# Layer 1's experts in two phases by choice, with residual and gates carried in the token's row, and shorter routing

## The reference

```python
gate_logits = x_flat @ Wg + bg + bias
topk_vals, topk_idx = jax.lax.top_k(gate_logits, 2)
topk_w = jax.nn.softmax(topk_vals, axis=-1)
h = relu(einsum('td,edh->teh', x_flat, W1) + b1)     # 256 -> 512
y = einsum('teh,ehd->ted', h, W2) + b2               # 512 -> 256
out = sum over the two chosen experts of topk_w * y
x = x + out
```

## Time and profile before

| what | value |
|---|---|
| runs without profile, us | 1401.55, 1405.42, 1402.47; median 1402.47 |
| the profiled execution's own time, us | 1402.67 |
| its span in the profile, us | 1400.8 |
| mean granted PE clock in the span, as a share of full | 0.828 |
| busy in the span: PE, DVE, POOL, ACT | 76%, 69%, 56%, 37% |
| layer 1's experts, first to last PE instruction, us from the start | 925 to 1325 |
| the combine after them | 1326 to the end |

### The profile page before, as it was taken

One profiled execution on the slowest core, in us unless ns is written; L12 is line 12 of the kernel. 1 busy time (PEld: TensorE's weight loads), 2 busy tenths in 40 slices (PEclk: granted clock), 3 DMA queues, 4 the chain that ended last, 5 costly groups with the idle time before them and its releaser, 6 DMA issues.

```text
span 1400.8 us, 30856 instructions
## 1 busy us (share of the span) xinstructions
PE 1061.8 (76%) x9022; PEld 875.1 (62%) x9023; DVE 965.6 (69%) x1758; ACT 520.3 (37%) x1067; POOL 784.7 (56%) x807
## 2 busy tenths in 40 slices
PE   5989756379999993667786481679999999999700
PEld 4767545248888882455564370459888888889600
DVE  3788689957777773578896798845555555555377
ACT  2656464802222221457676574012222222222200
POOL 3466755026666645777731375047777777777300
PEclk9999855559999997688888555569999999999955
DMA  9311124015555554333320253012222222223199
GB/s 284 56 46 39 61 95 146 0 30 159 165 165 165 165 143 128 87 112 114 117 61 31 90 171 115 1 57 91 93 91 90 90 91 93 94 90 93 52 356 363
DMA packets 121953, 157.13 MB, mean 112 GB/s; under 512 B 26904, under 2 KB 102176, under 8 KB 121632
## 3 DMA queue, kind: packets, MB, share of 16 engines
q1 hardware_dynamic: 96160, 86.05, 18.9%
q0 software_dynamic: 25728, 70.29, 17.0%
HBM read 95.47 MB, written 60.82 MB: 112 GB/s over the span
## 4 chain that ended last, share of the span: by engine, by line
PE 55%; issue 16%; DVE 12%; POOL 8%; DMA 4%; ACT 3%; SPq 1%; DVEq 0%; POOLq 0%; ACTq 0%
PE bank L814 19%; PE bank L828 19%; PE bank L785 5%; PE bank L797 4%; PE bank L663 4%; POOL WREG L534 3%; DMA arena<-expert_outputs 2%; DVE stats L1090 1%; DVE X L1100 1%; DVE X L1171 1%; SPq L306 1%; PE bank L691 1%; PE bank L681 1%; DVE X L1178 1%; POOL arena L542 1%
## 5 line engine op out<-in xcount | busy, mean ns | idle before, releaser
L605 POOL DMA_INDIRECT arena<-split_tokens,gather_row x272 | 282.0, 1037 | 233.9 <-DVE gather_row L1434 117.9
L1009 ACT ACTIVATE arena<-bank,b1T 128x256 f32<-128x256 f32 (+1 forms) x432 | 167.2, 462 | 497.1 <-PE bank L814 497.1
L828 PE MATMUL bank<-WREG,arena 128*128 x2448 | 289.8, 273 | 11.4 <-issue 5.2
L814 PE MATMUL bank<-arena,WREG 128*128 128x256 f16 (+1 forms) x2592 | 296.3, 269 | 0.0
L828 PEld LDWEIGHTS bank<-WREG,arena 128*128 128x128 f16 x2448 | 235.7, 98 | 47.5 <-issue 19.4
L814 PEld LDWEIGHTS bank<-arena,WREG 128*128 x2592 | 239.9, 99 | 26.5
L1446 DVE CAST arena<-arena 128x512 f16<-128x512 f32 (+1 forms) x136 | 78.7, 578 | 230.9 <-ACT arena L1009 230.9
L614 POOL DMA_INDIRECT expert_outputs<-arena,scatter_row x136 | 155.1, 1141 | 63.9 <-issue 40.6
L663 PE MATMUL bank<-wg_sb,arena 128*128 128x258 f32 x512 | 140.7, 422 | 41.4 <-ACT arena L874 33.6
L534 POOL DMA_INDIRECT WREG<-expert_outputs,pos_i x128 | 125.8, 983 | 61.0 <-issue 38.0
L663 PEld LDWEIGHTS bank<-wg_sb,arena 128*128 128x128 f32 x512 | 101.8, 208 | 65.3 <-issue 37.3
(11 more groups left out here) (190 smaller groups left out, 1343.4 us busy)
## 6 DMA issues: line engine op xcount, KB each, us to landing
expert_outputs<-arena SPq DMA_DIRECT2D x68, 256.0 KB, 2.8
split_tokens<-arena SPq DMA_DIRECT2D x32, 512.0 KB, 2.9
arena<-expert_outputs SPq DMA_DIRECT2D x32, 512.0 KB, 8.0
X<-in_x SPq DMA_DIRECT2D x16, 512.0 KB, 6.0
stage_w<-in_L_ffn_W SPq DMA_DIRECT2D x16, 512.0 KB, 3.4
out<-X SPq DMA_DIRECT2D x16, 512.0 KB, 8.0
arena<-split_tokens,gather_row POOLq DMA_INDIRECT x272
stage_w<-in_L_ffn_w SPq DMA_DIRECT2D x16, 256.0 KB, 2.8
```

The costliest lines, as they stand in the source:

```text
L605: nc.gpsimd.indirect_dma_start(out=gat[:, u * 512:(u + 1) * 512], out_offset=None, in_=table[L], in_offset=bass.IndirectOffsetOnAxis(ap=ga ...
L814: last = mm(hb, w1_at(L, ea, wh, kc, fc), tT[:, tb:tb + width], start=n == 0, stop=n == 3 * KC - 1)
L828: last = mm(ob[a], hsrc[:, h0:h0 + P], w2_at(L, e[a % len(e)], wh, fc), start=fc == 0 and n == 0, stop=fc == FC - 1 and n == 2)
L1009: ins = A(hid[:, h0:h0 + width], bank[2 + 2 * (u % 2) + fc // 2][:, b0:b0 + width], ACT.Gelu if L == 0 else ACT.Relu, bias=cut(b1T, ea * F ...
```

## The change

In both layers routing is trimmed: masks in float16, both choices' positions handled in one instruction where that can be (`pos_both`), one instruction instead of six from the matmuls' result to `gather_row`. The register loads of the slots' experts become one load for each slot, and the turn in layer 1 is eight slots long.

In layer 1 the two choices are routed apart. All first choices are one list (phase 0) and all second choices another (phase 1), each with room for 32 whole and 4 mixed slots: 72 slots, 144 tiles. Each token has one row of 2056 bytes in DRAM: the two float16 halves of y (1024 bytes), the residual x (1024 bytes) and the two gates (8 bytes). SP stores x into `token_rows_0` during the attention, y after the second layernorm; ACT stores the gates (8192 pieces of 8 bytes). In phase 0 a slot's rows are gathered from `token_rows_0` into a ring of 8 slots, which takes the place of X in SBUF; PE transposes the y part; when `copy_out` is done, DVE adds gate times output to the residual in the row (`add_to_row`, two instructions for a slot), and POOL scatters the whole row to `token_rows_1`. Phase 1 gathers from there, adds the second choice and scatters 1024 bytes to the result. There is no combine. Phase 1's rows can only be gathered when phase 0 is written (`phase_written`); for its first seven slots a second gather from `token_rows_0` (`fetch_early`) gives PE the y part sooner.

The diff, cut to what the prediction speaks of:

```diff
@@ constants
+PHASES = (1, TOPK)
+BIG = [TOKENS * TOPK // SLOT // n for n in PHASES]      # 64, 32
+RUN = [n + MIXED for n in BIG]                          # 68, 36
+SLOTS = [n * m for n, m in zip(PHASES, RUN)]            # 68, 72
+TURN = (SU, 2 * SU)
+ROW = 2 * D + TOPK
+RING = 2 * SU
+EARLY = 7
@@ def of_slots
-            eng.reg_load(regs, cut(table, first, len(regs)))
+            for f, r in slots:
+                mixed = isinstance(r, int) and r >= BIG[L]
+                key = f * KEYS[L] + (BIG[L] + ST * (r - BIG[L]) if mixed else r)
+                found.append([next(regs) for _ in range(ST if mixed else 1)])
+                eng.reg_load(found[-1], cut(table, key, len(found[-1])))
@@ SP
-        def load_outputs(sp, L):
...
+                def store_x(g):
+                    sp.wait_ge(x_done[1], at(4 * g + 4))
+                    sp.dma_start(rows_of(0)[:, g * GT:(g + 1) * GT, D:2 * D],
+                                 xs(g * GT, GT).rearrange("p (t d) -> p t d", d=D)).then_inc(x_stored, 16)
@@ POOL, layer 1
-                for t in range(AHEAD_G):
-                    gather(t)
-                for t in range(STILES):
-                    if t + AHEAD_G < STILES:
-                        gather(t + AHEAD_G)
-                    if L == 1:
-                        scatter(t)
+                def fetch(s):
+                    f, j = s // RUN[1], s % RING
+                    if s >= RING:
+                        pool.wait_ge(T_mm[1], at(s - RING + 1))
+                        pool.wait_ge(scattered[j], 16 * ST * (s // RING))
+                    for a in range(ST):
+                        nc.gpsimd.indirect_dma_start(
+                            out=token_row(ST * j + a, 0, ROW), out_offset=None, in_=token_rows[f],
+                            in_offset=bass.IndirectOffsetOnAxis(ap=gather_row[:, ST * s + a:ST * s + a + 1], axis=0)
+                        ).then_inc(rows_in[j], 16)
+                def scatter(s):
+                    f, j = s // RUN[1], s % RING
+                    pool.wait_ge(slots_ready[1], at(2 + f))
+                    pool.wait_ge(row_done[1], at(s + 1))
+                    for a in range(ST):
+                        to, start, n = ((out_rows, D, D) if f else (token_rows[1], 0, ROW))
+                        nc.gpsimd.indirect_dma_start(
+                            out=to, out_offset=bass.IndirectOffsetOnAxis(ap=scatter_row[...], axis=0),
+                            in_=token_row(ST * j + a, start, n), in_offset=None,
+                            bounds_check=TOKENS - 1, oob_is_err=False).then_inc(scattered[j], 16)
+                    pool.wait_ge(x_stored, 16 * GROUPS)
+                    pool.wait_ge(gates_stored, 16)
+                    R = RUN[1]
+                    for s in range(6):
+                        fetch(s)
+                    for s in range(R):
+                        scatter(s)
+                        if s + 6 < R:
+                            fetch(s + 6)
+                        if s + EARLY >= R:
+                            fetch_early(s + EARLY)
+                    phase_written()
+                    for s in range(R, R + 4):
+                        fetch(s)
+                    for s in range(R, 2 * R):
+                        scatter(s)
+                        if s + EARLY < 2 * R:
+                            fetch(s + EARLY)
+                        if s + 4 < R + EARLY:
+                            fetch(s + 4)
@@ PE
+                def slot(s, u, i, es):
+                    output(s, u, es[0])
+                    if u + 3 < SLOTS[L]:
+                        turn_over(s + 3, u + 3, i)      # layer 1: waits for rows_in, or early_in
+                    if u + 2 < SLOTS[L]:
+                        hidden(s + 2, u + 2, es[2])
@@ ACT
+                if L == 1:
+                    act.wait_ge(gates_ready[1], at(1))
+                    act.dma_start(rows_of(0)[:, :, 2 * D:ROW], gates[:]...).then_inc(gates_stored, 16)
@@ DVE
-                ch.mark(ts(inv_i, bank[2][:, 0:STILES].bitcast(I32), 16, None, ALU.arith_shift_right))
-                ch.mark(ts(inv_i, inv_i, EMPTY, None, ALU.subtract))
-                ch.mark(V.tensor_copy(inv_v, inv_i))
-                ch.mark(stt(inv_x, inv_v, float(-EMPTY), dump_id[:], ALU.is_equal, ALU.mult))
-                ch.mark(tt(scatter_row[:], inv_v, inv_x, ALU.add))
-                ts(gather_row[:].bitcast(I32), inv_i, TOKENS - 1, None, ALU.bitwise_and).then_inc(slots_ready[L], 1)
+                ts(gather_row[:, 0:STILES[L]].bitcast(I32), codes, 16, TOKENS - 1, ALU.arith_shift_right, ALU.bitwise_and).then_inc(slots_ready[L], 1)
+                def add_to_row(s, u, i, f):
+                    j = u % RING
+                    loop_wait(dve, o_ev[L], at(s + 1))
+                    loop_wait(dve, rows_in[j], i * (16 * ST) + 16 * ST * (u // RING + 1))
+                    for a in range(ST):
+                        o0 = (u % SU * ST + a) * D
+                        k = ST * j + a
+                        ins = stt(token_row(k, D, D), o_sb[:, o0:o0 + D], token_row(k, 2 * D + f, 1), token_row(k, D, D), ALU.mult, ALU.add)
+                    ins.then_inc(row_done[L], 1)
+                def slot(s, u, i, es):
+                    if u + 1 < SLOTS[L]:
+                        cut_hidden(s + 1, u + 1)
+                    copy_out(s, u, i, es[0])
+                    if u + 3 < SLOTS[L]:
+                        copy_T(s + 3, u + 3)
+                    if L == 1 and not (isinstance(s, int) and s < 2):
+                        add_to_row(s - 2, u - 2, i, ...)
-            combine(dve, ch, 1)
```

More of the change, by code:

```diff
@@ L283, in build, with of_slots @@
         slot_regs = {}
-        def of_slots(eng, table, i, n, per):
-            first = i * SU
-            mixed = [first + u >= BIG if isinstance(i, int) else False for u in range(n)]
+        def of_slots(eng, table, L, slots, per):
             if (eng, table.name) not in slot_regs:
[L290 to L293, removed]
-            eng.reg_load(regs, cut(table, first, len(regs)))
-            values = iter([eng.snap(r, min_val=0, max_val=(E - 1) * per) for r in regs])
-            return [(next(values), next(values)) if m else (next(values),) for m in mixed]
@@ new lines, in phase, with all_slots, by_number @@
+        def phase(s, L, more=0):
+            return [(n // RUN[L], n % RUN[L]) for n in range(s, min(s + more, SLOTS[L]))]
+        def all_slots(eng, L, table, per, ahead, slot, apart=()):
+            def by_number(f, first, last):
+                for s in range(f * RUN[L] + first, f * RUN[L] + last, SU):
+                    es = of_slots(eng, table, L, phase(s, L, SU + ahead), per)
+                    for u in range(SU):
+                        slot(s + u, s + u, 0, es[u:u + ahead + 1])
+            for f in range(PHASES[L]):
+                T = TURN[L]
+                begin = 1 if f in apart else 0
+                by_number(f, 0, begin * T)
+                with eng.Fori(begin, TURNS[L]) as i:
+                    es = of_slots(eng, table, L, [(f, i * T + u) for u in range(T + ahead)], per)
+                    for u in range(T):
+                        slot(f * RUN[L] + i * T + u, f * RUN[L] + u, i, es[u:u + ahead + 1])
+                by_number(f, TURNS[L] * T, RUN[L])
@@ L362, in _ @@
                     sp.sem_inc(y_stored[h][L], 16)
+            for u in range(SU):
+                sp.sem_inc(stored[u], 16)
             def load_gnn(L):
@@ L436, in _ @@
                 if L == 0:
-                    for s in range(SLOTS):
+                    for s in range(SLOTS[0]):
                         u = s % SU
@@ L1011, in activate @@
                     ins.then_inc(h_act[L], 1)
-                def experts(i, more):
-                    es = of_slots(act, slot_expert, i, SU + (2 if more else 0), 1)
-                    for u in range(SU):
-                        if more or u + 2 < SU:
-                            activate(i * SU + u + 2, u + 2, es[u + 2])
+                def slot(s, u, i, es):
+                    if u + 2 < SLOTS[L]:
+                        activate(s + 2, u + 2, es[2])
+                if L == 1:
+                    act.wait_ge(gates_ready[1], at(1))
+                    with nc.allow_non_contiguous_dma(reason="two gates at the end of each token's row"):
+                        act.dma_start(rows_of(0)[:, :, 2 * D:ROW], gates[:].rearrange("p (t k) -> p t k", k=TOPK)).then_inc(gates_stored, 16)
                 act.wait_ge(slots_ready[L], at(1))
-                first = of_slots(act, slot_expert, 0, 2, 1)
+                first = of_slots(act, slot_expert, L, phase(0, L, 2), 1)
                 for s in range(2):
                     activate(s, s, first[s])
-                with act.Fori(0, TURNS - 2) as i:
-                    experts(i, True)
-                experts(TURNS - 2, True)
-                experts(TURNS - 1, False)
+                all_slots(act, L, slot_expert, 1, 2, slot)
         @block.vector
```

448 lines of the change are left out of this document (232 added, 216 removed).

## The result

The changed kernel takes 1645.42 us (median; 1644.27 to 1646.53), 1.172 times the kernel before (95% interval 1.1704 to 1.1742; before in the same job 1403.66). The profiled execution has a span of 1642.5. So it is slower, as forecast, but by 242 us instead of 109, and outside the range. In two later jobs (e1 to e8) the kernel before took 1402 to 1403 again. In the last two (e9 to e12) it took 1587 and 1596, so their totals can be set only beside each other.

The account below looks back on a forecast made before the run. PE sets the pace in layer 1's experts; token loads, additions and stores fill the last 74.9 us. 1402.67 - 65 + 153 + 14 + 4 - 4.6 + 3 + 3 + 1 = 1511 us; range 1474 to 1562.

Parts of the forecast that it names:

- Smaller things: Small costs: layer 0's register loads +3 us (0 to 22), stores of x +1, gates' 8192 pieces nothing (end +20).
- The loop: Layer 1's phase 0: the fetch behind the waiting scatter makes a slot 10.0 us (9.0 to 10.9), 129 us more.
- POOL wakes: 0.28: Phase 0 loop term: POOL starts the scatter 0.28 us after DVE's addition releases it.
- I add 0.4, an estimate: Phase 0 loop term: rows of 2056 instead of 1024 bytes land 0.4 us later.
- The collision: Phase 0 loop term: the second fetch meets DVE's cast or subtraction and ends about 0.7 us later.
- Rival B: Phase 0: PE's clock stays at the lower level, 11.3 us a slot, 39 us more, 1550; chance 0.12.
- Rival C: POOL's issue time doubles with 2056-byte rows or the bounds check: 1661 us, half of it 1586; chance 0.12.
- Rival A: Phase 0: PE never waits for rows, 1373 us; the change wins below 6.4 us a slot; chance 0.06.
- The phase change: Layer 1, from phase 0 to phase 1: PE waits 8 us, then 2 more in each of three rounds; +14 (5 to 20).
- Phase 1: Layer 1's second choices: a loop over two slots just at PE's pace, plus collisions; +4 us (0 to 15).
- The combine: End of the kernel: last additions and six scatters take 10 us instead of 74.9; -65.
- Routing: Ahead of the experts in both layers: trims save 4.6 us in layer 0, layer 1 takes 3 more.

Follow-up runs that it names:

- e1: Changed kernel with all register loads of one turn joined into one load; 1563.65 us, ratio 1.1149.
- e8: e4 with the wait for the scatter's rows moved out of the scatter, done once ahead of phase 0; 1412.17 us, ratio 1.0069.
- e9: Changed kernel with one register load for a turn on PE only, single loads on ACT and DVE; 1720.9 us, ratio 1.0849 (kernel before 1587).
- e12: Same kernel as e9, run again in another job; 1713.49 us, ratio 1.0733 (kernel before 1596).
- e2: Kernel before with one register load for each slot, nothing else of the change; 1492.99 us, ratio 1.0643.
- e7: Kernel before with a bounds check on its scatter, with a bound that no row reaches; 1402.34 us, one run.
- e11: e1 with layer 1's fetches reading 1024-byte rows from layer 0's table; 1683.9 us in a job with a slow kernel before, 10.44 a slot in phase 0.
- e4: Changed kernel with one register load for each turn and phase 0's fetch ahead of the scatter; 1412.3 us, ratio 1.0077.

## Why the prediction was right in its direction and wrong in its size

**The step that failed: "Smaller things", the register loads.** The prediction took 0.2 us a turn, 3 us in all, with 22 as the end. Runs e1 and e2 measured 82 and 90. The first error is the price. I read the 0.30 idle of the earlier trace rows as an upper bound for a load, and allowed five times that. Five more loads on each engine lengthen PE's pause by 2.3 us in layer 0, 0.46 for each, and that is more than the 0.30 that one load and the branch left together. So part of the one load's time was presumably hidden before; that was not tried. Behind the pauses the clock falls, which no term and no rival of the prediction had for layer 0: 1.3 more a turn, 20 us in all. Together it is 3.6 a turn, most of it by PE's own loads (e9: 16.4 - 13.5 = 2.9). The second error is the count: I multiplied by layer 0's 15 turns alone. Layer 1's turns pay too (30.5 against 25.3 for slots 0 to 5, 255.5 against 240.5 for 35 to 71), 25 us together. This one term is 79 of the 134 us that the forecast was off. The rest is in e1's column: 35 in the loop, 13.5 from slot 35 to 71 and 5 at the end.

**The loop was right, 10.0 was not.** That it binds is shown twice over: PE and POOL wait as foretold in each slot, and putting the fetch ahead gives 134 to 151 us back; "129" for the loop becomes 148 as measured. Of its terms the transposes, copy, additions and issues held within 0.1. Two were mis-sized. "POOL wakes: 0.28" was 0.88: a row of a scatter without a bounds check was used for one with it (e7). "I add 0.4, an estimate" for the longer rows was 0.7 to 0.9 (e11): the 0.4 is the growth of one gather (0.8 less 0.4), and a slot has two. The collision is there but is 0.3 in most slots, 0.7 in some. Together 10.6 for the quick slots and 11.16 on average. The Trainium skill (SBUF — State Buffer, The DMA setup-cost knee) gives a transfer 2 us and its bytes over 436 GB/s. By that two gathers would grow by 0.6, an estimate from that page; e11's trace has 0.67 behind the end of the second one's instruction.

**Rival B** did not come. The clock fell to 0.80 in phase 0, from the 1.00 of the earlier trace rows, but PE still waited for rows 97 us in 27 slots, so it was not the bound; some slots pay 0.4 for transposes at half clock, as the forecast had it. **Rival C** was wrong: POOL's time for a DMA is the same with 2056 bytes and with the check. **Rival A's** condition was made by hand in e4, 6.22 us for a slot, below the 6.4 from which the prediction let the change win, and it still loses by 10 us. The break-even left out what else was mis-sized: the tail (14.5 instead of 10), the phase change and phase 1.

**The phase change**, "Sum 14": the intervals up to slots 43 to 47 in e1 are 15.5, 7.8, 8.8, 7.0 and 6.9, which is 17 over five of 5.8; within the ends of 5 and 20. PE waited 7.7 where I worked out 8; the rounds behind it took 2.1 and 3.1 more rather than 2. The seven intervals between the loop and the stall (slots 35 to 42) hold another 5 that the forecast did not have.

**Phase 1**, "+4, ends 0 and 15": in e1 slots 47 to 71 take 149.2, 6.2 each, so about 10 over 5.8. POOL is busy 116.7 of 170 us in the second window above, and 104 pauses of 0.30 make it 148: four DMAs of 1.3 and the collisions come close to PE's pace. That this is the cause was not tried.

**The combine**, -65: measured -60.4. The scatters went out as foretold (8.3 for 7.5). The end of the program lies 6.2 behind the last one's start, where I had only the landing of 2.4; what fills the rest the records don't show.

**Routing**, -4.6 and +3: layer 0's experts begin 4.0 sooner (303.94), and layer 1's routing takes 77.2 (900.82 to 978.0) for 75.4, 1.8 more. Both are near. The gates' 8192 pieces landed in 13.2 us, with the first fetch behind them, and cost nothing, as forecast. The stores of x cost 2 us at most: slot 0 of layer 1 comes at 926.6 in e1, for 924.7 without the term for the loads.

## What to carry to other kernels

Before costing an edit at nothing because "PE may run ahead", look at what its sequencer has to finish first: at the head of a loop's turn each further register load held TensorE up for 0.4 to 0.5 us here, and in layer 0 the clock that fell behind the pause added half as much again. So load all of a turn's values in one instruction. When a pause appears, read the granted clock of the stage beside it, or the price of the pause and that of the clock are taken for one. When a queue with one order feeds a loop, draw the loop and price it with the changed instructions, not with their nearest kin before; and put what feeds the bound engine ahead of what waits. Try the cheap parts of a large change alone: the routing trims gave 0.55%, the rest took it away many times over.

## What the runs showed of the hardware

- Five register loads more at the head of a turn left TensorE idle for 2.6 us in one piece in layer 0, where a single load of several registers left 0.30, and for 1.8 in layer 1 (e2), where the kernel before loses 0.1 at a turn's head.
- With those pauses of 2.6 the granted clock of layer 0's stage was 0.91, without them 0.98 (e1), and the same matmuls took some 20 us more. With the pauses of 1.8 in e2's layer 1 it stayed at 1.00.
- A bounds check on an indirect DMA delays its start after a wait by 0.52 us (0.28 to 0.80). It lengthens neither the instruction (0.98) nor the 0.30 in front of one that doesn't wait. A second wait that is already satisfied costs 0.06.
- With rows of 2056 bytes instead of 1024, a slot's two gathers of 128 rows each reach PE 0.86 us later (3.71 to 2.85 from the second gather's start, 2.50 to 1.83 from its end), while an undisturbed issuing instruction takes 1.0 for both.
- The Trainium skill (SBUF — State Buffer, on who interferes with whom) has DVE and GpSimd share one port pair as an exclusive lock. The trace agrees: a fetch that starts in DVE's cast takes 1.25 and ends 0.84 behind it, and 0.97 to 0.99 without one. A fetch that starts in DVE's subtraction is held in the same way, up to 1.69. By the page, whoever starts first has the ports for the whole instruction. There the trace differs: POOL's DMA instructions that started 0.25 to 0.55 ahead of a cast were held too and ended 0.12 to 0.14 behind it (e11's row above: from 1156.63 to 1157.87, the cast from 1157.06 to 1157.75).
